# Per-token q·k sums in a gated linear attention kernel: a token-stationary product or an indicator-stationary one

## The reference

```python
def _gla_scan(q, k, v, g):
    S0 = jnp.zeros((q.shape[-1], v.shape[-1]), q.dtype)
    def step(S, inp):
        qt, kt, vt, gt = inp
        S = jnp.exp(gt)[:, None] * S + kt[:, None] * vt[None, :]
        return (S, qt @ S)
    return jax.lax.scan(step, S0, (q, k, v, g))[1]
...
q = (x @ Wq) * HK ** -0.5;  k = x @ Wk;  v = x @ Wv
g = log_sigmoid(x @ gk_w1 @ gk_w2 + gk_b) / 16.0
o = gla_scan(q, k, v, g)                        # for each head
o = o * rsqrt(mean(o * o) + EPS) * rms_w
o = o * silu(x @ Wg);  y = o @ Wo
...
x = x + layernorm(y);  h = gelu(layernorm(x) @ w1 + b1);  x = x + layernorm(h @ w2 + b2)
```

## Time and profile before

| | |
|---|---|
| median of 3 runs | 1358.65 us (1355.38 to 1363.46) |
| the profiled execution | 1360.29 us, of these 1358.6 us span |
| TensorE busy | 1275.6 us, 94% |
| VectorE busy | 1034.3 us, 76% |
| ScalarE busy | 712.5 us, 52% |
| GpSimd busy | 634.6 us, 47% |
| mean granted TensorE clock | 0.966 of 2.4 GHz |

### The profile page before, as it was taken

The page is one execution under the profiler, slowest core; times in us unless marked ns, Lnnn a source line. Parts: engine busy times, 40 slices in busy tenths (PEclk is TensorE's granted clock), DMA queues, the critical chain, the costliest instruction groups (busy, mean ns, idle before and its releaser), DMA issues.

```text
span 1358.6 us, 26477 instructions
## 1 busy us (share of the span) xinstructions
PE 1275.6 (94%) x8388; PEld 1122.6 (83%) x8388; DVE 1034.3 (76%) x2404; ACT 712.5 (52%) x1427; POOL 634.6 (47%) x889
## 2 busy tenths in 40 slices
PE   5889999999998999999999999999999999999967
PEld 3678889788897888888888788987889788898956
DVE  3669787786977868768787787877787786978763
ACT  5365555645455465644655446564555645455423
POOL 4436354544444544544445635355353543545541
PEclk9989999989999999989999899998999989999988
DMA  2000010100101001010011001010010100101000
GB/s 94 36 32 17 17 48 9 52 10 17 47 21 49 1 17 48 24 45 1 17 48 52 18 17 41 8 51 18 17 48 5 48 17 17 48 21 32 1 16 16
DMA packets 31797, 38.54 MB, mean 28 GB/s; under 512 B 2448, under 2 KB 29104, under 8 KB 31664
## 3 DMA queue, kind: packets, MB, share of 16 engines
q1 hardware_dynamic: 31136, 36.25, 7.9%
q10 hardware_dynamic: 528, 0.52, 0.1%
HBM read 28.38 MB, written 8.39 MB: 27 GB/s over the span
## 4 chain that ended last, share of the span: by engine, by line
PE 75%; DVE 10%; issue 7%; DVEq 0%; POOL 0%; ACT 0%; POOLq 0%
PE ps_big L261 14%; PE ps_big L263 13%; PE ps_big L262 13%; PE ps_level L304 12%; PE ps_out L453 5%; PE ps_out L456 3%; PE ps_level L261 3%; DVE attn_T L576 3%; DVE q_blockdiag L586 2%; PE ps_level L263 2%; PE ps_level L262 2%; PE ps_transpose L467 2%; PE ps_transpose L277 2%; PE ps_state L435 2%; DVE h_lo L591 2%
## 5 line engine op out<-in xcount | busy, mean ns | idle before, releaser
L304 PE MATMUL ps_level<-q_blockdiag,k_decayed 128*128 128x128 f32 x1792 | 282.5, 295 | 26.4 <-issue 16.1
L304 PEld LDWEIGHTS ps_level<-q_blockdiag,k_decayed 128*128 128x128 f32 x1792 | 247.7, 201 | 52.8 <-issue 32.8
L1041 POOL TENSOR_TENSOR k_decayed<-k_decayed,block_totals 128x256 f32<-128x256 f32 x192 | 168.3, 876 | 259.5 <-PE ps_level L304 259.5
L576 DVE COPY_PREDICATED attn_T<-level_masks,ps_level 128x512 f32<-128x512 uint32 x160 | 152.8, 955 | 27.2 <-PE ps_level L304 23.7
L1047 POOL TENSOR_TENSOR rstd<-rstd,minus_half 128x1 f32<-128x1 f32 x192 | 114.2, 595 | 117.7 <-DVE rstd L638 116.4
L586 DVE TENSOR_TENSOR q_blockdiag<-q_blockdiag,block_totals 128x512 f32<-128x512 f32 x192 | 147.3, 768 | 27.4 <-PE ps_level L304 27.4
L838 ACT ACTIVATE gelu_out<-ps_big,ff_b_cols 128x512 f32<-128x512 f32 x128 | 88.1, 688 | 130.9 <-PE ps_big L263 97.9
L261 PE MATMUL ps_big<-w_ff_hi,h_hi 128*128 128x256 f32 x512 | 150.2, 293 | 2.7 <-DVE h_lo L591 2.7
L263 PE MATMUL ps_big<-w_ff_hi,h_lo 128*128 128x256 f32 x512 | 144.9, 283 | 0.0
L262 PE MATMUL ps_big<-w_ff_lo,h_hi 128*128 128x256 f32 x512 | 144.7, 283 | 0.0
L624 DVE SCALAR_TENSOR_TENSOR o<-o,o_rstd,out_gate 128x128 f32<-128x128 f32 x256 | 91.3, 418 | 46.1 <-POOL o_rstd L1063 46.1
(11 more groups left out here) (110 smaller groups left out, 3291.7 us busy)
## 6 DMA issues: line engine op xcount, KB each, us to landing
w_raw<-L_ffn_w SPq DMA_DIRECT2D x16, 1024.0 KB, 5.2
out<-y SPq DMA_DIRECT2D x16, 512.0 KB, 2.9
x_in<-L_attn_x SPq DMA_DIRECT2D x15, 512.0 KB, 3.4
ff_b_rows<-L_ffn_b SPq DMA_DIRECT2D x8, 128.0 KB, 2.0
x_in<-L_attn_x ACTq DMA_DIRECT2D x1, 512.0 KB, 4.0
w_raw<-L_attn_Wv SPq DMA_DIRECT2D x1, 512.0 KB, 5.5
w_raw<-L_attn_Wg SPq DMA_DIRECT2D x1, 512.0 KB, 6.5
y<-L_attn_Wo SPq DMA_DIRECT2D x1, 512.0 KB, 7.5
```

The lines of the kernel that those rows point to most:

```text
L304: last = nc.tensor.matmul(PL[tl][:, c * CH:(c + 1) * CH], kk[:, tl, c * CH:(c + 1) * CH], q[:, :, :, 1, :], start=True, stop=True)
L576: nc.vector.copy_predicated(dst, m.to_broadcast([P, 2 * NCH, HC // h, h]), src)\
L1041: nc.gpsimd.tensor_tensor(k, k, t.to_broadcast([P, T // (2 * h), h]), ALU.mult)\
```

## The change

The indicator becomes the stationary operand, and `q_times_k` moves. `head_sum` has 32 columns for each tile, zero but for two. `diag_rows` issues 8 products behind level 0: for each tile and chunk c, 128 columns of `q_times_k` move through the 32 stationary columns, and the result lands in partitions 32c to 32c+31 of `ps_out`; the two tiles are summed there. Row 32c+h holds head h of chunk c. ScalarE copies the 128x128 result into the first columns of `o`, which is free at that time. `diag_columns`, behind step 3, transposes it on TensorE into columns 128 to 255 of `ps_out`, and VectorE takes the 16 useful columns ahead of its step 4.

```diff
-        ind = sb("head_sum", [P, 2])
+        ind = sb("head_sum", [P, KT, 32])
...
-                        if i == 0:
-                            self_product = diag(c, tl)
                     last.then_inc(sem["pe_lv"], 1)
-                    if i + 1 == tl:
-                        self_product.then_inc(sem["pe_diag"], 1)
-
-                def diag(c, tl):
-
-                    w = c * H + 2 * tl
-                    return nc.tensor.matmul(PO[:, w:w + 2], qk[:, tl, c * CH:(c + 1) * CH], ind[:, :],
-                                            start=True, stop=True)
+
+                def diag_rows():
+
+                    for tl in range(KT):
+                        for c in range(NCH):
+                            last = nc.tensor.matmul(PO[32 * c:32 * (c + 1), 0:CH], ind[:, tl, :],
+                                                    qk[:, tl, c * CH:(c + 1) * CH], start=(tl == 0), stop=(tl == KT - 1))
+                    last.then_inc(sem["pe_drow"], 1)
+
+                def diag_columns():
+                    pe.wait_ge(sem["ac_dg"], at("ac_dg", s, 1))
+                    nc.tensor.transpose(PO[:, CH:2 * CH], o[:, 0, 0:CH], ident[:, :]).then_inc(sem["pe_diag"], 1)
...
                         level(step // 2, step % 2)
+                        if step == 1:
+                            diag_rows()
+                        if step == 3:
+                            diag_columns()
...
-                    if B and step == 1:
+                    if B and step == 4:
                         dve.wait_ge(sem["pe_diag"], at("pe_diag", s, 1))
-                        nc.vector.tensor_copy(dg[:, :], PO[:, 0:NCH * H]).then_inc(sem["dv_dg"], 1)
+                        nc.vector.tensor_copy(dg[:, :].rearrange("p (c h) -> p c h", h=H),
+                                              PO[:, CH:2 * CH].rearrange("p (c r) -> p c r", r=32)[:, :, 0:H])\
+                            .then_inc(sem["dv_dg"], 1)
...
+                if B:
+                    act.wait_ge(sem["pe_drow"], at("pe_drow", s, 1))
+                    copy(o[:, 0, 0:CH], PO[:, 0:CH], "ac_dg")
                 if C:
                     for kt in range(KT):
                         act.wait_ge(sem["pe_x3t"], at("pe_x3t", p, kt + 1))
...
-                fill(ind[:, :], QSCALE)
-                select(ind[:, 0:1], [[0, 1]], HK - 1, -1)
-                select(ind[:, 1:2], [[0, 1]], -HK, 1)
+                fill(ind[:, :, :], 0.0)
+                for tl in range(KT):
+                    pool.wait_ge(c_step, count[0])
+                    fill(ind[:, tl, 2 * tl:2 * tl + 2], QSCALE)
+                    select(ind[:, tl, 2 * tl:2 * tl + 1], [[0, 1]], HK - 1, -1)
+                    select(ind[:, tl, 2 * tl + 1:2 * tl + 2], [[0, 1]], -HK, 1)
```

More of the change, by code:

```diff
@@ L134, in build @@
             pe_xt=KT, pe_gl=KT, pe_k=KT, pe_q=KT, pe_v=NCH, pe_g=NCH,
-            pe_diag=1, pe_lv=2 * NL, pe_kt=2, pe_st=NCH - 1, pe_att=NCH, pe_ogt=NCH, pe_wo=NCH,
+            pe_drow=1, pe_diag=1, pe_lv=2 * NL, pe_kt=2, pe_st=NCH - 1, pe_att=NCH, pe_ogt=NCH, pe_wo=NCH,
             pe_x3t=KT, pe_f1=FT, pe_f2=NCH,
@@ L152, in build @@
             ac_xhi=KT, ac_abs=KT, ac_e=1, ac_l=1, ac_a=1, ac_k=KT, ac_v=NCH, ac_g=NCH, ac_qb=2 * KT,
-            ac_cp=6, ac_kt=2, ac_sq=NCH * H, ac_oghi=NCH,
+            ac_cp=6, ac_dg=1, ac_kt=2, ac_sq=NCH * H, ac_oghi=NCH,
             ac_x3hi=KT, ac_gelu=FT, ac_hhi=FT, ac_ws=2,
```

## The result

The changed kernel takes 1337.6 us (median of 4 runs, 1337.32 to 1340.01); the kernel before took 1360.19 us beside it. The ratio is 0.9841, with a 95% interval of 0.9807 to 0.9874: 1.6% faster, where 1.2% was forecast. In two later sets, on chips of their own, the same two kernels stood at 0.9863 (0.9843 to 0.9883) and 0.9862 (0.9838 to 0.9886).

What follows compares the result with a forecast made beforehand. TensorE was taken as the bound behind the loop's jump, VectorE in even stages; 0.9 + 0.7 + 0.8 + 13.2 = 15.6 us gained, 1344.7 from 1360.3, or 1343 against the median of 1358.65; range 1334 to 1354.

Steps and rivals of the forecast that it cites:

- The clock: Sequences 3 to 13: dense level 0 brings 2.4 GHz about 3.5 us behind the restart, at times 7; chance 0.56.
- The rival that the clock comes back no sooner: Six stages behind the jump gain only 0.9 us each; in all 8 us, time 1350.5 (1347 to 1355); chance 0.23.
- The added TensorE work: TensorE: 16 new matmuls with 32 stationary columns cost 0.95 us including two switches; bounds 0.68 and 2.15.
- no overlap: Column groups don't overlap, added part costs 2.15 us; the six stages gain about nothing, time 1356; chance 0.10.
- the reason given for it: New matmuls on TensorE: consecutive instructions of one float32 product share a column group; no size of its own.
- Behind the jump: Sequence 5, restart to level 2: 10.1 us instead of 13.07, 2.9 gained; the six such stages together 13.2 us.
- the sum (6.68 + 0.68 + 0.7): Sequence 5, first masked copy to level 2: 6.68 base, 0.68 for q's slower update, 0.7 waiting for transposes' copies.
- The deduction of 2.5 us for late returns of the clock: Six stages behind the jump: 2.5 us taken off their gain where the clock comes back one step later.
- Even stages: Sequences 2 to 14, and 15: TensorE's saving becomes waiting; only VectorE's 0.11 us per stage stays, 0.9 us in all.
- `k_update` starts earlier and was nobody's bound: GpSimd's update of k: its earlier start was to change nothing, 0 us.
- Sequences 0 and 1: First two sequences: 0.7 us gained in sequence 0 and 0.8 us in sequence 1.
- The clock falling in even stages: Rival: longer TensorE waits ahead of steps 3 and 4 drop the clock in eight stages, +27 us, time 1370; chance 0.06.

Runs made afterwards that it cites:

- experiment 1: Kernel before, with the two-column products moved as a block behind level 0 and VectorE's 16-column copy ahead of its step 4: 1343.28 us, ratio 0.9902.
- experiment 2: Kernel before, products left in between, but each moving 128 columns (zero-padded indicator) instead of 2: 1345.28 us, ratio 0.9913.
- experiment 3: Changed kernel, with the eight two-column products put back between level 0's products, results read by nobody: 1361.28 us, ratio 1.0014.
- the two repetitions: Two repeated profiles of the changed kernel, nothing altered; its two later sets stood at 0.9863 and 0.9862.
- experiment 4: Changed kernel, with the new products ordered chunk by chunk, so neighbours share a column group: 1340.47 us, ratio 0.9871.
- experiment 5: Changed kernel, with GpSimd's first update of k waiting for VectorE's last x_normed: 1341.19 us, ratio 0.9882.
- experiment 6: Changed kernel, GpSimd's first k update waiting for the last x_normed, its second for VectorE's first q update: 1339.65 us, against 1339.48 for the changed kernel.
- experiment 8: The two waits of experiment 6 in even stages only: on the changed kernel 1335.00 us, on experiment 1's kernel 1339.24; changed kernel beside them 1338.70.
- experiment 7: Kernel of experiment 1 (two-column products as a block, no column groups) with the two waits of experiment 6: 1339.26 us, ratio 0.9861.

## Why the prediction was right

*The clock: right, and the main step.* It was argued from two stages of one trace, with a chance of 0.56. Experiments 1, 2 and 3 take it apart: with the products moved away or widened the half-speed stretches were short, with the products put back they were 10.2 us again. The forecast of 3.4 us, at times 6.8, was too careful: 3.4 in all six here, and in the two repetitions three and two of the six stages had no half-speed stretch at all. The rival that the clock comes back no sooner is out.

*The added TensorE work: mechanism right, size too large.* Forecast 0.95 us. It is read best where the clock is at 2.4 GHz throughout and the transposes don't wait for `x_normed`, in sequence 5 of the first repetition:

```profile
430.73 2.08 PE L304 MATMUL ps_level<-q_blockdiag,k_decayed 128*128 128x128 f32 x16 [2.90 <-issue]
432.74 0.65 PE L313 MATMUL ps_out<-q_times_k,head_sum 128*32 128x128 f32 x16
433.32 1.09 PE L277 MATMUL ps_transpose<-ident,x_normed 128*128 128x128 f32 x8
```

The last matmul of level 0 starts at 430.73 + 2.08 - 0.275 = 432.54 and the transposes at 433.32; less the 0.11 us between neighbours that is 0.67 us, at the lower bound of 0.68. The matmuls themselves start four at a time, 16 in (0.64 - 0.273) = 0.37 us, a little under the quarter price (0.45) in that bound. Their rival, no overlap, is out. So is the reason given for it: which group the neighbour uses doesn't matter (experiment 4).

*Behind the jump: 2.9 us forecast for sequence 5, 3.6 measured.* Restart to level 2 was to be 10.1 us and is 9.6 to 10.0, in part by luck. In sequence 5 the first masked copy starts 2.93 us behind the restart, not 2.05, since `x_normed` itself starts later and takes 1.03 us; and from there to level 2 it is 7.1 us, not the 8.1 of the sum (6.68 + 0.68 + 0.7), since VectorE doesn't wait for the transposes' copies, and its update of q for level 1 takes 0.87 us, no longer 1.41. The two errors cancel. Another 0.5 us of the gain came behind level 2, where the next update of q takes 0.72 us instead of 1.37; why wasn't tried. The deduction of 2.5 us for late returns of the clock wasn't needed. Of 13.2 us forecast for the six, 20.8 came.

*Even stages: wrong in sign.* "Only the 0.11 us stays" failed; 0.1 to 0.8 us were lost instead, in sequences 2 to 14. The step that failed is "`k_update` starts earlier and was nobody's bound". It was true of the wait and missed the collision: an instruction of an engine off the path now starts just ahead of one of VectorE, which is on it, and the latter takes 0.93 us instead of 0.41. Experiments 5, 6 and 8 show this: the instruction falls back to 0.41 us, and with both collisions avoided the stages take 8.6 to 8.7 us, what 8.8 less 0.11 would be. That TensorE's saving turns into waiting was right (0.74 and 0.56 us where 0.35 was), and experiment 7 agrees.

*Sequences 0 and 1*: 1.5 us forecast, 0.6 measured from level 0 of sequence 0 on, 2.7 with what lies ahead of it. In sequence 1 level 2 came 0.94 us sooner and 0.66 of this was lost again by the last level. By which instruction wasn't tried.

*The clock falling in even stages*: it didn't in sequences 2 to 14, in any profile, nor in sequence 15 in the three of the changed kernel. The risk was there all the same: in sequence 15 TensorE waits 1.40 and 0.56 us ahead of steps 2 and 3, and in experiment 4, the same kernel but for an order, a half-speed stretch of 3.4 us followed at 1235.1 us and level 2 came 10.8 us behind level 0 instead of 9.8. Experiments 6 and 8 (the waits on the changed kernel) have one there too.

The span shrank by 22.8 us where 15.6 had been forecast. The six stages gave 7.6 us more than forecast, the even ones 3.1 less, the time up to level 0 of sequence 2 1.2 more, and sequence 15 with what follows it 1.5 more, which the repetitions don't show. That the gain as a whole missed by 7 us and not by more owes something to these signs.

## What to carry to other kernels

A float32 matmul that moved two columns through 128 stationary ones cost nearly the time of one that moved 128, and with such matmuls in between TensorE's clock stayed at 1.2 GHz three times as long behind a stop. Look at what stands in the first microseconds behind each stop of the loop. Work that an engine off the path starts earlier has to be checked for what it now runs beside: here it was VectorE's `tensor_scalar` and two-input instructions beside GpSimd's. Where a saving on one engine turns into its waiting, moving the work can be worth more than making it cheaper: here the move gave some 14 us, and the cheaper product nothing (experiment 7) to 5.

## What was not expected of the hardware

Float32 matmuls with 32 stationary columns in four column groups start four at a time (within 0.02 us in the order of the change, 0.04 in that of experiment 4), and the rounds are 0.11 to 0.13 us apart in both orders. In experiment 1 TensorE restarted at full speed, and the clock fell 5.4 us later for 3.4 us, behind the block of two-column products and a wait of 0.31 us. Whether the stop of 2.39 us or the block brought it down stays open.
